# Longer rows for two streams of stores: the zero fill of a sum buffer, and the edge filters

## Chip, cores, metric
The kernel runs on one core of one Trainium2 chip. The metric is the device time of one execution in microseconds; the time given for a kernel is the median of its runs.

## What is computed
A graph of 10000 nodes with 512 features and 10000 edges goes through two layers, each with a residual and a normalisation over the features.

```python
def layer0(x):                      # graph convolution
    deg = segment_sum(w_all, dst_all);  norm = rsqrt(deg)[src] * w * rsqrt(deg)[dst]
    return relu(segment_sum((x @ W)[src_all] * norm, dst_all) + b)
x = layernorm(x + layer0(x))
def layer1(x):                      # message passing with edge filters
    h = softplus(edge_attr_20 @ Wf1 + bf1) - log 2
    filt = (h @ Wf2 + bf2) * edge_weight          # depends on the edges alone
    m = products of x[dst] @ W_in, edge directions and filt
    agg = segment_sum(m, src)                     # then small matrices per node
x = layernorm(x + layer1(x))
```

## The kernel before, in words
Edges and nodes are worked in tiles of 128 (79 live tiles; tensors are padded to 80). Five engines have an order of instructions each, written out by hand and tied by semaphores.

**Opening.** SP issues the small loads, then 33 fills of 512 KB (L421) and one of 256 KB (L422) that set `sum0` in HBM to zero; ScalarE's queue issues the first eight (`NZ`, L640). The source is `zeros`, 128 x 1024 fp32, so each fill writes 4 KB from each partition into two neighbouring rows of 2 KB. VectorE makes `zeros` by its first memset (L883). Meanwhile TensorE, VectorE and ScalarE compute the node degrees, and POOL gathers the first 12 tiles of x rows (L536).

**First edge stage** (some 84 to 340 us). A loop over groups `g` of four tiles: ScalarE and VectorE scale the gathered rows by the edge coefficient and split them into a high and a low part, TensorE sums rows with equal destination inside the group, ScalarE copies the sums to `R_mem` (L685), and POOL adds them to `sum0` by four indirect scatters (L552), then gathers four tiles for three groups later (L536). The scatters of a group wait until all of the group before have landed (`e_scat`), for the index columns that VectorE makes (`e_idx`, L991), and for the copy (`e_ev`). The first scatter also waits for the whole zero fill (`s_zero0`). In the same loop the filters of the second layer are made, since they depend on the edges alone: two tiles at a time, TensorE forms them (L1255), ScalarE writes them to `wst` (in `node_mem`, L679), and SP stores the pair to `filt_d` in HBM (L434), two stores of 512 KB per group. `wst[i % 4]` holds 128 partitions x 2 tiles x 512; the store puts tile v of the pair at rows 128 v + p, so that each row of 2 KB goes to a place of its own, 256 KB from the partition's other one.

**Node stage** (340 to 600 us), once all scatters have landed: x @ W0 and the first normalisation. **Second edge stage** (600 to 950 us): a loop over tiles with gathers, products, sums and scatters; SP loads the filter of tile t by `filt_in` (L456, 256 KB, four buffers), three tiles ahead. **Last stage**: the second normalisation and the output.

`keep` (128 x 6144) holds W0 in its first 2048 columns and, from the node stage on, part of x1.

Of the kernel before, what the change touches and what calls it, by code (L numbers as in the profile page):

```python
# [13 lines left out]
P = 128  # L14
# [3 lines left out]
D = 512  # L18
# [39 lines left out]
def place(t):  # L58

    g = (t + 2) // 3  # L60
    return g, t - first(g)
# [40 lines left out]

def rows(dram, t):
    return dram[bass.ds(t * P, P), :]


def pair_rows(dram, s, c0, c1):

    return dram[bass.ds(s * 2 * P, 2 * P), c0:c1].rearrange("(k p) d -> p k d", p=P)


def layer_pair(dram, j, c0, c1):
# [13 lines left out]
def build(nc, x, src_cols, dst_cols, src_row, weight, rbf, vec,  # L126
          W0, b0, Win_s, Win_v, Wf1, bf1, Wf2, bf2, W1_s, W1_v, W2_s, W2_v, out):
    sum0 = nc.dram_tensor("sum0", (NR + TRASH, D), F32, kind="Internal").ap()
    sum1 = nc.dram_tensor("sum1", (NR + TRASH, D), F32, kind="Internal").ap()
    x1_d = nc.dram_tensor("x1_d", (NR, D), F32, kind="Internal").ap()  # L130
    filt_d = nc.dram_tensor("filt_d", (NP, D), F32, kind="Internal").ap()

    with ExitStack() as ctx:
        def sb(name, shape, dt=F32):
            return ctx.enter_context(nc.sbuf_tensor(name, shape, dt))

        def sem(name):
            return ctx.enter_context(nc.semaphore(name))
# [7 lines left out]
        zeros = sb("zeros", [P, 1024])  # L146
# [33 lines left out]
        keep = sb("keep", [P, 24 * 2 * C])  # L180
# [26 lines left out]
        def views(start, n, width, mem=edge_mem):  # L207
            return [mem[:, start + i * width:start + (i + 1) * width] for i in range(n)]
# [24 lines left out]
        NG = 12  # L233
        G0 = G + [b[:, 2 * D:3 * D] for b in node_mem]
        junk1 = [b[:, 3 * D:3 * D + 3 * P] for b in node_mem]
        W0_s = [keep[:, c * D:(c + 1) * D] for c in range(4)]
        pick_even = views(0, 4, P)
        sl2 = [b[:, 0:2 * D] for b in node_mem]
# [7 lines left out]
        wst = [b[:, 0:1024].rearrange("p (v d) -> p v d", v=2) for b in node_mem]  # L246
        filt = [b[:, 0:512] for b in node_mem]
# [31 lines left out]
        s_zero = sem("s_zero")  # L279
        s_zero0 = sem("s_zero0")  # L280
# [63 lines left out]
        w_st = [sem(f"w_st{i}") for i in range(4)]  # L344
        w_dup = sem("w_dup")
        w_sidx = sem("w_sidx")
        f_filt = [sem(f"f_filt{i}") for i in range(4)]
# [32 lines left out]
        NZ = 8  # L380

        def zero_rows(j):
            return sum0[j * 256:(j + 1) * 256, :].rearrange("(p r) d -> p (r d)", r=2)
# [10 lines left out]

        minus = before[:, 0:P]

        block = ctx.enter_context(nc.Block())


        @block.sync  # L400
        def _(sp_):
# [14 lines left out]

            for s in range(2):
                sp_.dma_start(fT[s][:, :], rbf[:, s * Q:(s + 1) * Q]).then_inc(w_fT[s], 16)
            sp_.wait_ge(s_zero, 1)
            for j in range(NZ, 41):  # L420
                sp_.dma_start(zero_rows(j), zeros[:, :]).then_inc(s_zero0, 16)  # L421
            sp_.dma_start(sum0[41 * 256:, :], zeros[:, 0:D]).then_inc(s_zero0, 16)  # L422
            for c in range(4):
                sp_.dma_start(W0_s[c], W0[c * P:(c + 1) * P, :]).then_inc(s_wres, 16)
# [2 lines left out]
            for s in range(2, T4 + 3):  # L427
                if s < T4:
                    sp_.wait_ge(w_pre, s - 1)
                    sp_.dma_start(fT[s % 2][:, :], rbf[:, s * Q:(s + 1) * Q]).then_inc(w_fT[s % 2], 16)  # L430
                if s >= 3:
                    for i in (2 * (s - 3), 2 * (s - 3) + 1):
                        sp_.wait_ge(w_eva, 4 * (i + 1))
                        sp_.dma_start(pair_rows(filt_d, i, 0, D), wst[i % 4]).then_inc(w_st[i % 4], 16)  # L434


            sp_.wait_ge(e_lo, T)
# [15 lines left out]
                   .then_inc(f_trow[g % 4], 16)  # L453

            def filt_in(t):
                sp_.dma_start(filt[t % 4], rows(filt_d, t)).then_inc(f_filt[t % 4], 16)  # L456

            def nodes0(j):
                if j < T2:
                    if 1 <= j < 4:  # L460
                        x_in(j)
                    wait(sp_, n_tr, 2 * j - 6)
                    sp_.dma_start(in_pair(sl2[j % 4], j, 0, D), layer_pair(sum0, j, 0, D)).then_inc(n_sl[j % 4], 16)
                    if j == 4:
                        sp_.wait_ge(s_pairs, 1)
                    if j >= 8:
                        sp_.wait_ge(n_sum, 2 * j - 14)
                    if j >= 4:
                        x_in(j)
                if j >= 6:  # L470
                    i = j - 6
                    sp_.wait_ge(n_x1, min(2 * i + 2, TR - 2))
                    if i >= T2 - 2:
                        sp_.wait_ge(n_last, i - T2 + 3)
                    sp_.dma_start(layer_pair(x1_d, i, 0, D), in_pair(res2[i % 8], i, 0, D)).then_inc(n_st[i % 8], 16)
                    if i < T2 - 4:
                        sum1_out(i)
                    if i == T2 - 3:
                        sp_.wait_ge(n_tr, TR)
                        trow_in(0)  # L480
                        filt_in(0)
# [7 lines left out]
            for t in range(1, 4):  # L489
                filt_in(t)  # L490
                trow_in(t)
# [5 lines left out]
            for s in range(4, TR):  # L497
                g, j = place(s)
                if j == 0 and g >= 4:
                    sp_.wait_ge(f_M, first(g - 3))  # L500
                    trow_in(g)
                sp_.wait_ge(f_m, K_PROD * (s - 3))
                filt_in(s)
# [8 lines left out]
            for s in range(T2 + NA - 3):  # L512
# [4 lines left out]
                if s >= NA - 3:  # L517
                    t = s - NA + 3
# [8 lines left out]
        def _(pool):  # L527
# [6 lines left out]
            def gather0(t):  # L534
                k = t % NG
                pool.indirect_dma_start(G0[k], None, x, bass.IndirectOffsetOnAxis(ap=src_i[:, t:t + 1], axis=0)) \  # L536
                    .then_inc(e_gather[k // 4], 16)

            pool.wait_ge(s_load, 64)
            for t in range(NG):  # L540
                gather0(t)
            pool.wait_ge(s_zero0, 16 * 42)
            for g in range(T4):
                pool.wait_ge(e_idx, 2 * (g + 1))
                if g:
# [1 line left out]
                for n, j in enumerate((3, 2, 1, 0)):  # L547
                    t = 4 * g + j
# [44 lines left out]
            for g in range(G1 + 5):  # L593
# [7 lines left out]
                if g >= 5:  # L601
                    r = g - 5
# [272 lines left out]
        def _(dve):  # L875
# [5 lines left out]
                dve.wait_ge(s_const, count[0])  # L881

            dve.memset(zeros[:, :], 0.0).then_inc(s_zero, 1)  # L883
            dve.memset(eps_c[:, :], EPS)
            dve.memset(half_c[:, :], 0.5)
            dve.wait_ge(s_iota, 4)
# [48 lines left out]
            for s in range(T4 + 1):  # L935
# [18 lines left out]
                if s >= 1:  # L954
                    dve.wait_ge(s_look, g + 1)
                    for v in range(4):
                        t = 4 * g + v
# [16 lines left out]
                if s >= 1:  # L974
# [3 lines left out]
                    for q in (3, 2, 1, 0):  # L978
                        t, w = 4 * g + q, (q + 1) * P
                        dve.tensor_scalar(M[a][q], trow[a][:, 0:w], dst_f[:, t:t + 1], None, ALU.is_equal).then_inc(e_M, 1)  # L980
                    for n, q in enumerate((3, 2, 1, 0)):
                        t = 4 * g + q
# [26 lines left out]
            for q in range(2):  # L1009
                k = Y0 / (16.0 * C ** 0.5) if q == 0 else 1.0 / (16.0 * C ** 0.5 * 3.0 ** 0.5)  # L1010
# [7 lines left out]
            for k in range(2):  # L1018
                for half in range(2):
                    i = 2 * k + half  # L1020
# [65 lines left out]
            for t in (TR - 2, TR - 1):  # L1086
                g, k, r = t // 2, t % 2, res[t % 16]
# [378 lines left out]
```

## Time and profile before

| what | us |
|---|---|
| median of 3 runs (lowest, highest) | 1063.95 (1062.75, 1065.17) |
| the profiled execution | 1060.8 |
| its span from first to last instruction | 1058.7 |
| TensorE, VectorE, ScalarE, POOL busy | 943.4, 837.9, 703.7, 642.6 |
| SP's fills of `sum0`: first issue | 18.55 |
| shortest gather and shortest scatter on POOL | 0.95, 1.55 |

The span is what the views cover; the execution's own time holds some 2.1 us around it. A DMA share is the mean busy share of the core's 16 DMA engines in a stretch; overlapping packets can take it over 1. In a timeline the bracket gives how long the engine stood idle before the instruction, and what ended that by the semaphore events. A wait for several semaphores is put down to the last one that the profile saw.

### The profile page before, as it was taken

What the parts mean: (1) busy time and instruction counts of PE and PEld (TensorE: products, weight loads), DVE (VectorE), ACT (ScalarE), POOL (GpSimd) and SP (SyncE); (2) the same over time, 40 slices, a digit from 0 to 9 for tenths busy, and PEclk for the clock granted to TensorE, in tenths of its full rate; (3) what the DMA queues carried; (4) which work ended last, traced back from release to release, by engine and by line L of the source; (5) the groups of instructions that cost most, each with busy time, mean ns of one, the idle gap of its engine ahead of it and who ended that gap; (6) DMA issues with size and microseconds to landing.
All of it is one profiled execution on the core that took longest, in us unless ns stands there. A gap on an engine that the chain in (4) does not pass through costs nothing.

```text
span 1058.7 us, 17984 instructions
## 1 busy us (share of the span) xinstructions
PE 943.4 (89%) x5218; PEld 767.6 (73%) x5218; DVE 837.9 (79%) x2368; ACT 703.7 (66%) x1641; POOL 642.6 (61%) x931
## 2 busy tenths in 40 slices
PE   5979999898894999999999679999999999929885
PEld 4958777776673788888888457887888888818774
DVE  5778788887662789888888758888888888817998
ACT  2668877787682466666666645666666666618997
POOL 4017888888863356666666354676666766534664
PEclk9989999999896999999999889999999999969998
DMA  9989999999998599988999586999999999768999
GB/s 346 418 303 223 247 238 237 237 238 238 231 236 192 217 321 331 331 318 318 334 327 331 223 295 166 220 227 213 206 222 229 215 206 218 122 102 329 410 416 365
DMA packets 105703, 280.43 MB, mean 265 GB/s; under 512 B 13107, under 2 KB 17479, under 8 KB 105607
## 3 DMA queue, kind: packets, MB, share of 16 engines
q1 hardware_dynamic: 68598, 191.42, 49.3%
q0 software_dynamic: 35280, 82.63, 40.7%
q10 hardware_dynamic: 1728, 5.24, 1.3%
q8 instruction: 43, 0.70, 0.3%
q14 instruction: 54, 0.43, 0.1%
HBM read 132.38 MB, written 146.87 MB: 264 GB/s over the span
## 4 chain that ended last, share of the span: by engine, by line
PE 55%; DMA 6%; DVE 5%; issue 2%; ACT 1%; POOL 1%; SPq 0%; DVEq 0%; POOLq 0%; ACTq 0%
PE bank L1330 14%; PE bank L1334 7%; PE bank L1378 7%; PE bank L1361 7%; PE bank L1392 5%; PE bank L1390 3%; PE bank L1321 3%; PE bank L1355 3%; DVE stat L1168 2%; PE bank L1388 2%; PE bank L1367 2%; DMA out<-R_mem 1%; DMA sum<-R_mem,l_sidx 1%; PE bank L1365 1%; PE bank L1356 1%
## 5 line engine op out<-in xcount | busy, mean ns | idle before, releaser
L552 POOL DMA_INDIRECT sum<-R_mem,sidx_all x79 | 131.3, 1662 | 91.1 <-DMA sum<-zeros 49.3
L613 POOL DMA_INDIRECT sum<-R_mem,l_sidx x79 | 134.6, 1704 | 48.3 <-DMA sum<-R_mem,l_sidx 25.3
L1330 PE MATMUL bank<-G_hi 128*128 128x512 f32 x316 | 130.4, 413 | 0.0
L599 POOL DMA_INDIRECT G_mem<-x_d,dst_i x79 | 77.3, 979 | 87.3 <-PE bank L1365 61.5
L1330 PE MATMUL bank<-G_lo,G_hi 128*128 128x512 f32 x316 | 124.2, 393 | 0.0
L1244 PE MATMUL bank<-G_hi,M_mem 128*128 128x512 f32 x200 | 85.4, 427 | 9.4 <-ACT R_mem L685 9.4
L1334 PE MATMUL bank<-G_hi,G_lo 128*128 128x512 f32 x316 | 85.3, 392 | 0.0
L1119 DVE SCALAR_TENSOR_TENSOR edge_mem<-edge_mem,Y,bank 128x128 f32<-128x128 f32 x237 | 71.2, 385 | 15.1 <-ACT edge_mem L806 14.1
L1361 PE MATMUL bank<-edge_mem,Winv 128*128 128x512 f32 x158 | 81.8, 600 | 0.1
L1244 PE MATMUL bank<-G_lo,M_mem 128*128 128x512 f32 x200 | 79.6, 398 | 0.0
L1255 PE MATMUL bank<-edge_mem,Wf_s 128*128 128x256 f32 x320 | 78.6, 390 | 0.7 <-ACT node_mem L679 0.7
L754 ACT CAST G_hi<-bank 128x512 fp32r<-128x512 f32 x79 | 45.7, 579 | 40.5 <-PE bank L1321 40.2
L679 ACT ACTIVATE node_mem<-bank,bf_c 128x256 f32<-128x256 f32 x160 | 63.3, 490 | 13.5 <-issue 7.3
L1255 PEld LDWEIGHTS bank<-edge_mem,Wf_s 128*128 128x128 f32 x320 | 63.5, 201 | 11.6 <-issue 2.9
L584 POOL TENSOR_TENSOR node_mem<-node_mem,G_mem 128x512 f32<-128x512 f32 x40 | 53.6, 1339 | 28.9 <-ACT node_mem L768 28.9
L536 POOL DMA_INDIRECT G_mem<-x,src_i x55 | 58.2, 1059 | 20.7 <-issue 12.8
L1378 PE MATMUL bank<-G_hi,M_mem 128*128 128x512 f32 x157 | 68.4, 436 | 2.5 <-ACT R_mem L800 2.2
L1334 PEld LDWEIGHTS bank<-G_hi,G_lo 128*128 128x128 f32 x316 | 59.3, 188 | 13.1
L1330 PEld LDWEIGHTS bank<-G_lo,G_hi 128*128 128x128 f32 x316 | 59.6, 189 | 10.6
L1330 PEld LDWEIGHTS bank<-G_hi 128*128 128x128 f32 x316 | 59.5, 188 | 10.1
L1392 PE MATMUL bank<-MV,edge_mem 128*128 128x128 f32 x474 | 65.8, 275 | 0.0
L806 ACT COPY edge_mem<-bank 128x256 f32<-128x256 f32 x79 | 29.5, 373 | 53.9 <-issue 32.7
(263 smaller groups left out, 2921.2 us busy)
## 6 DMA issues: line engine op xcount, KB each, us to landing
node_mem<-sum SPq DMA_DIRECT2D x41, 512.0 KB, 5.9
filt_d<-node_mem SPq DMA_DIRECT2D x40, 512.0 KB
node_mem<-filt_d SPq DMA_DIRECT2D x79, 256.0 KB
sum<-zeros SPq DMA_DIRECT2D x33, 512.0 KB
G_mem<-x SPq DMA_DIRECT2D x20, 512.0 KB, 6.3
x_d<-node_mem SPq DMA_DIRECT2D x20, 512.0 KB, 2.9
sum<-node_mem SPq DMA_DIRECT2D x20, 512.0 KB, 4.5
edge_mem<-x SPq DMA_DIRECT2D x19, 512.0 KB, 6.3
```

The source lines that it names most:

```text
L552: pool.indirect_dma_start(sum0, bass.IndirectOffsetOnAxis(ap=sidx[:, t:t + 1], axis=0), R[t % 8][:, :], None, compute_op=ALU.add).then_inc ...
L599: pool.indirect_dma_start(G3[t % 8][:, :], None, x1_d, bass.IndirectOffsetOnAxis(ap=dst_i[:, t:t + 1], axis=0)) \
L613: pool.indirect_dma_start(sum1, bass.IndirectOffsetOnAxis(ap=l1_sidx[0:n, t:t + 1], axis=0), R3[t % 8][0:n, :], None, compute_op=ALU.add). ...
L679: act.activation(wst[i % 4][:, :, q * P:(q + 1) * P], bank[6 + q // 2][:, (q % 2) * 256:(q % 2 + 1) * 256].rearrange("p (v e) -> p v e", v=2),
L1119: st.mark(dve.scalar_tensor_tensor(mo[:, :, i], msg[c][:, 0:P], Y[:, bass.ds(t, 1), i], bank[6][:, i * P:(i + 1) * P], ALU.mult, ALU.add))
L1244: ins = pe.matmul(bank[b][:, :], M[c][q][:, j * P:(j + 1) * P], part_[(4 * g + q) % 8][:, :], start=(q == 3 and part_ is G_hi), stop=(q == ...
L1255: ins = pe.matmul(bank[6 + r][:, q * 256:(q + 1) * 256], Wf2_s[:, base:base + 255:2], h[c][:, v * 256:(v + 1) * 256], start=True, stop=True)
L1330: pe.matmul(bank[4 + a][:, :], zT_hi[a][:, c * P:(c + 1) * P], w[c][:, :], start=(c == 0 and w is W0h), stop=False)
L1334: ins = pe.matmul(bank[4 + a][:, :], zT_lo[a][:, c * P:(c + 1) * P], W0h[c][:, :], start=False, stop=(c == 3))
L1361: pe.matmul(bank[2][:, :], Winv[:, :], rawT[b][:, 0:512], start=True, stop=True)
L1378: ins = pe.matmul(bank[sum_bank[k]][:, :], M3[g % 3][j][:, k * P:(k + 1) * P], part_[t % 8][:, :], start=(k == j and part_ is msg_hi), sto ...
L1392: ins = pe.matmul(bank[6][:, i * P:(i + 1) * P], m[b][:, (3 + i) * P:(4 + i) * P], MV[:, 1, :], start=True, stop=True)
```

## The change
It has two parts. (1) A second memset makes `zeros_8k`, 2048 columns of zeros in columns 2048 to 4095 of `keep`. SP's 32 fills of 512 KB become 16 of 1 MB with 8 KB from each partition to four neighbouring rows; the 33rd, the 256 KB one and ScalarE's eight stay. SP waits for both memsets, and POOL for the new number of fills. (2) The two tiles of a filter pair are stored with their rows side by side: partition p's rows of tile 2i and 2i+1 are rows 256 i + 2p and 256 i + 2p + 1 of `filt_d`, so that a partition writes 4 KB in one piece. The load of a tile then reads every second row.

```diff
-def pair_rows(dram, s, c0, c1):
-    return dram[bass.ds(s * 2 * P, 2 * P), c0:c1].rearrange("(k p) d -> p k d", p=P)
...
+        zeros_8k = keep[:, 4 * D:8 * D]
...
+        def filt_pair(i):
+            return filt_d[i * 256:(i + 1) * 256, :].rearrange("(p v) d -> p v d", v=2)
...
-            sp_.wait_ge(s_zero, 1)
-            for j in range(NZ, 41):
-                sp_.dma_start(zero_rows(j), zeros[:, :]).then_inc(s_zero0, 16)
+            sp_.wait_ge(s_zero, 2)
+            for j in range(NZ // 2, 20):
+                sp_.dma_start(sum0[j * 512:(j + 1) * 512, :].rearrange("(p r) d -> p (r d)", r=4), zeros_8k).then_inc(s_zero0, 16)
+            sp_.dma_start(zero_rows(40), zeros[:, :]).then_inc(s_zero0, 16)
             sp_.dma_start(sum0[41 * 256:, :], zeros[:, 0:D]).then_inc(s_zero0, 16)
...
-                        sp_.dma_start(pair_rows(filt_d, i, 0, D), wst[i % 4]).then_inc(w_st[i % 4], 16)
+                        sp_.dma_start(filt_pair(i), wst[i % 4]).then_inc(w_st[i % 4], 16)
...
-                sp_.dma_start(filt[t % 4], rows(filt_d, t)).then_inc(f_filt[t % 4], 16)
+                sp_.dma_start(filt[t % 4], filt_pair(t // 2)[:, t % 2, :]).then_inc(f_filt[t % 4], 16)
...
-            pool.wait_ge(s_zero0, 16 * 42)
+            pool.wait_ge(s_zero0, 16 * (NZ + 18))
...
             dve.memset(zeros[:, :], 0.0).then_inc(s_zero, 1)
+            dve.memset(zeros_8k, 0.0).then_inc(s_zero, 1)
```

## Rows read from the trace of the kernel before

**Rows 1.** The page: busy time of each engine, and the count of DMA packets.
```profile
PE 943.4 (89%) x5218; PEld 767.6 (73%) x5218; DVE 837.9 (79%) x2368; ACT 703.7 (66%) x1641; POOL 642.6 (61%) x931
...
DMA packets 105703, 280.43 MB, mean 265 GB/s; under 512 B 13107, under 2 KB 17479, under 8 KB 105607
```

**Rows 2.** By stretch: length, engines' busy time, granted clock, DMA share, GB/s.
```profile
30.00:64.00 34.00, 29.85 (x128) 26.43 (x128) 22.91 (x92) 22.68 (x57) 0.00 (x0) 1.00 1.03 419
...
100.00:300.00 200.00, 182.22 (x889) 141.58 (x887) 158.13 (x578) 157.05 (x323) 163.23 (x120) 0.98 1.02 241
...
640.00:940.00 300.00, 293.02 (x1846) 235.50 (x1844) 254.34 (x735) 190.40 (x441) 193.11 (x140) 0.99 0.92 199
```

**Rows 3.** Timeline of POOL, first scatters: start, duration, instruction, idle before.
```profile
70.41 1.64 POOL L552 DMA_INDIRECT sum<-R_mem,sidx_all  x1 [49.30 <-DMA sum<-zeros]
...
79.03 1.55 POOL L552 DMA_INDIRECT sum<-R_mem,sidx_all  x1 [5.09 <-ACT R_mem L685]
```

**Rows 4.** Timeline of VectorE: memset, first work on loads, first index columns.
```profile
1.02 0.91 DVE L883 MEMSET zeros<- 128x1024 f32 x1 [1.02 <-PEq L1460]
...
5.67 0.20 DVE L891 CAST src_f<-src_i 128x80 f32<-128x80 int32 x1 [3.42 <-DMA rij<-vec]
...
69.44 0.16 DVE L991 TENSOR_TENSOR sidx_all<-off_all,dst_f 128x4 int32<-128x4 f32 x1
```

**Rows 5.** DMA view from 317.0 to 318.4 us.
```profile
DMA packets 259, 0.51 MB, mean 367 GB/s; under 512 B 8, under 2 KB 8, under 8 KB 259
...
q1 hardware_dynamic: 259, 0.51, 98.1%
```

**Rows 6.** DMA view from 30 to 64 us.
```profile
DMA packets 3904, 14.23 MB, mean 419 GB/s; under 512 B 434, under 2 KB 434, under 8 KB 3902
...
q1 hardware_dynamic: 3902, 14.21, 102.4%
```

**Rows 7.** Timeline of POOL in the first edge stage.
```profile
117.43 1.62 POOL L552 DMA_INDIRECT sum<-R_mem,sidx_all  x1 [0.30 <-issue]
...
123.10 1.99 POOL L552 DMA_INDIRECT sum<-R_mem,sidx_all  x1 [0.30 <-issue]
...
130.81 1.62 POOL L552 DMA_INDIRECT sum<-R_mem,sidx_all  x1 [0.30 <-issue]
...
297.26 1.55 POOL L552 DMA_INDIRECT sum<-R_mem,sidx_all  x1 [0.30 <-issue]
...
303.68 1.62 POOL L552 DMA_INDIRECT sum<-R_mem,sidx_all  x1 [0.71 <-issue]
```

**Rows 8.** By stretch, POOL with VectorE busy and with VectorE idle.
```profile
84.80:87.60 2.80, 2.80 (x14) 2.45 (x13) 2.61 (x9) 2.80 (x7) 2.39 (x2) 1.00 0.94 131
316.90:324.20 7.30, 6.28 (x29) 5.02 (x27) 0.00 (x0) 4.08 (x10) 6.23 (x4) 1.00 0.94 212
```

**Rows 9.** Timeline of POOL at the stage's end; last row: the chain of waits.
```profile
309.61 2.09 POOL L552 DMA_INDIRECT sum<-R_mem,sidx_all  x1 [0.30 <-issue]
316.99 1.56 POOL L552 DMA_INDIRECT sum<-R_mem,sidx_all  x1 [5.29 <-ACT R_mem L685]
...
322.58 1.56 POOL L552 DMA_INDIRECT sum<-R_mem,sidx_all  x1 [0.30 <-issue]
329.63 1.56 POOL L552 DMA_INDIRECT sum<-R_mem,sidx_all  x1 [5.50 <-issue]
...
333.36 5.75 DMA sum<-R_mem,sidx_all
```

**Rows 10.** The filter loads (L456): starts, and who waited for them.
```profile
L456 SPq DMA_DIRECT2D node_mem<-filt_d x79: 319/320/1595, 601.4 to 910.8; - x79
...
  DVE edge_mem L1128: 0.3, 1
```

**Rows 11.** Timeline of TensorE in the opening.
```profile
18.75 0.72 PE L1217 MATMUL bank<-hot_hi,hot_mem 128*128 128x80 f32 x2 [1.21 <-issue]
21.92 0.69 PE L1217 MATMUL bank<-hot_hi,hot_mem 128*128 128x80 f32 x2 [2.45 <-issue]
```

## The prediction
> **What bounds the kernel now.** I read the page first. TensorE is busy 943.4 of 1058.7 us, VectorE 79%, POOL 61% [rows 1]: near full on the whole, and an average says nothing of a single stage. The table by stretch does [rows 2]. From 345 us on, where the node and the second edge stage run, TensorE is the full one (293.02 of 300 us from 640 to 940) and the change touches only the reads of the filters there. The change works ahead of that: the zero fill (30 to 64 us: DMA share 1.03, 419 GB/s) and the first edge stage, where the filters are stored (100 to 300 us: share 1.02 at only 241 GB/s, TensorE 182 of 200). So the question is what sets the pace of these two.
>
> The timeline of POOL answers the first [rows 3]. Its first scatter starts at 70.41 after 49.30 us of idling that the profile puts down to the zeros. That looks like a 49 us prize, and is none: the index that the same scatter needs is written by VectorE at 69.44 for 0.16 us, to 69.60 [rows 4]. With the usual 0.30 us of dispatch the scatter could start at 69.90 at best. The third then waits 5.09 us for a sum that ScalarE copies, whose inputs come from TensorE and VectorE and not from the fill. From 84 us on POOL issues without a gap: in its timeline each instruction is preceded by 0.30 us of dispatch and hardly ever more, up to 310 us [rows 7], in groups of four scatters and four gathers, 13.38 us each (117.43 to 130.81). The stage then ends in three groups without gathers between them, where POOL waits for the scatters before to land, 5.29 and 5.50 us, and the last landing, 5.75 us, releases the node stage [rows 9]. That is what the end hangs on: POOL's issuing, then three landings.
>
> **The change, part by part.**
> *The wider memset.* VectorE's memset of 1024 columns takes 0.91 us, so one of 2048 takes about 1.82. It stands behind the first, in front of work that waits until 5.67 us for a load with 3.42 us of idling [rows 4]. Cost 0; without that cover it would be 1.82 us, and I see none of it left. SP's wait for it is free too: SP comes to it only after its weight loads, at 18.55 us (the table above).
>
> *What a packet costs.* From 317.0 to 318.4 us hardly anything but filter stores was under way: 98.1% of 16 engines for 1.40 us over 251 packets of 2 KB (259 less 8 small ones) are 87.5 ns each [rows 5]. From 30 to 64 us the queue carried 4 KB packets: 102.4% of 16 engines for 34 us over 3468 are 160.6 ns [rows 6]. Two of 2 KB cost 175.0, so a pair saves 14.4 ns, 8.2%. A store of 512 KB has 16 packets an engine now (1.40 us) and then 8 (1.285): 0.115 us less each, 0.23 us for the two of a group, 4.6 us for all 40. The other bound is 0, if what limits is bytes or if the long rows go out in pieces.
>
> *The zero fill.* 32 fills of 512 KB become 16 of 1 MB, 4 KB rows become 8 KB ones. The 32 take 32 x 1.285 = 41.1 us of full engines. No row shows an 8 KB data packet. The lower bound is 0. The upper takes the same 14.4 ns off each pair: 2 x 160.6 - 14.4 = 306.8 instead of 321.2 ns, 4.5%, 1.85 us. I take the nearer half of that, about 1 us, as true of the fill, and 0.0 on the path: only 0.51 us of it can reach the first scatter (70.41 to 69.90), and the third scatter's 5.09 us of idling take that up. ScalarE's eight fills keep their rows.
>
> *The filter stores in the stage.* They lie beside POOL's issuing. In steady groups the last scatter ends its issue at 123.10 + 1.99 = 125.09 and the next group's first starts at 130.81; less 0.30 of dispatch that is a cover of 5.42 us for the landing [rows 7]. At 303.68, with three gathers between, the landing shows through: 298.81 to 303.38, 4.57 us, with 0.71 us of idling instead of 0.30. So a faster store buys at most 0.41 there, and the like in the few other groups that show more than 0.30; I take 0.2 in all. Is POOL itself held up by the DMA? Its scatters take 1.55 us at least and up to 2.09 [rows 9]. While VectorE was idle and the DMA full of scatters and stores (316.9 to 324.2, share 0.94) four of them took 6.23 us, the minimum each; while VectorE was busy and the DMA moved 131 GB/s (84.8 to 87.6), two gathers took 2.39 us together where 0.95 is the least for one [rows 8]. The stretched ones go with the engines' work rather than with the DMA. So 0 from there.
>
> *The tail.* Two of the three landings, 311.70 to 316.69 (4.99 us) and 324.14 to 329.33 (5.19), have stores among them; the last has none [rows 9]. If two stores' packets stand ahead of each, they save 0.23 us each: 0.46.
>
> *The reads.* 79 loads of 256 KB keep their 2 KB rows, now 4 KB apart in memory. A row of 2 KB is its own packet either way. Only 0.3 us of waiting in the whole stage is put down to them [rows 10], and they are asked for three tiles ahead, some 11.9 us when 79 of them start from 601.4 to 910.8, 3.97 us apart. Cost 0; a cost would need loads that take several us more.
>
> **The sum.** 0 (memset) - 0 (fill) - 0.2 (loop) - 0.46 (tail) = about -0.7 us. In the profiled execution 1060.8 us (span 1058.7 and 2.1 around it) becomes 1060.1. The runs' median stands 3.15 us above it, at 1063.95, and becomes 1063.3.
>
> What the Trainium skill says of packets, in "DMA: Bandwidth & Descriptors" under "Why small descriptors are slow", is an overhead of about three cycles on a packet of one cycle per 32 bytes: 134 cycles for two of 2 KB against 131, 2.2% where the rows show 8.2%. By it a store would save an estimated 0.03 us and the sum would be about -0.2.
>
> **The rivals.**
> *The DMA sets the pace of the stage (faster).* For it: share 1.02 over 200 us, and a period of 13.38 us that is hardly more than the DMA could do. Against it: the two stretches of [rows 8] and a POOL that never idles. The 17 groups between 84 and 310 us would each give back 0.23, 3.9 us, the tail 0.46: 1063.95 - 4.4 = 1059.5.
>
> *Longer turns of the stores (slower).* A store's packets alternate with those of the scatters on each engine. Where a scatter's eight packets per engine take turns with a store's, each now waits behind 160.6 ns instead of 87.5: 8 x 0.073 = 0.58 us later landing. In steady groups the landing (5.19 in the tail) has 0.23 us to spare under the cover of 5.42, so 0.35 us show in each group in which the last scatter meets a store, and 0.58 in two landings of the tail. In all 17 groups that makes 6.0 + 1.2 = 7.2 us, in half of them 4.2: 1068.2. It decides once a landing takes over 5.42 us. Against it: the store's total work shrinks, and a store that meets the first three scatters delays the last one no more than now. The skill's rule for this is in the same page, "Queues, rings and completion order": an engine goes round its queues a packet at a time. The trace shows stores and scatters in the same stretches but not their turns.
>
> *Longer turns of the fill (slower).* TensorE stood 1.21 and 2.45 us at 18.75 and 21.92 us for nothing that the profile shows, with the DMA full [rows 11]. If code or some other small transfer is what it waits for, and packets of the fill are twice as long, these could double: +3.7, 1067.6. Against it: the same full DMA from 25 to 64 us shows no such gaps, and the fill only begins at 18.5.
>
> *The packets don't change.* If rows of 4 and 8 KB go out in the old pieces, nothing moves: 1063.95.
>
> **How the numbers follow.** Forecast 0.52; packets unchanged 0.10; DMA pace 0.20; turns of the stores 0.13; turns of the fill 0.05. Runs of this kernel lie within 1.2 us of their median, and 0.2% (2.1 us) is about what can be told from no change. Of the forecast's own spread (1061.5 to 1065.0) I put 0.03 beyond on the faster and 0.02 on the slower side. Faster by over 0.2%: 0.20 + 0.03 = 0.23. Slower: 0.13 + 0.05 + 0.02 = 0.20. Same: 0.57. The range reaches down to the DMA-bound case, 1059.5, and up to 1067.0, short of the two slower ones.
>
> **What the profile after would show.** Packets fewer by 40 x 128 = 5120 for the stores and 16 x 128 = 2048 for the fill (105703 to about 98,500) if the rows go out whole. The first scatter at 69.9 to 70.4, the third where it was. POOL's period still near 13.4 us with 0.30 ahead of each instruction; if it drops to 13.15, the DMA was the bound and I am wrong. Landings of 4.8 to 5.0 us in the tail; 5.5 and more with idling ahead of each group's first scatter would be the longer turns. The stages from 340 us on the same length: a longer one would speak against the reads.

## The result and the profile after

The changed kernel takes 1068.4 us (median of 6, 1066.67 to 1070.46) against 1063.14 us for the kernel before in the same series (6 runs): a ratio of 1.0049, 95% interval 1.0035 to 1.0063. It is about 5 us slower, outside the stated range (1059.5 to 1067.0) and on the side that was given 0.20. The rival "longer turns of the stores" had named 1068.2, from a start at 1063.95.

The page after, beside [rows 1]; lines behind L885 have moved by one, L552 has not:

```profile
span 1067.4 us, 17969 instructions
...
PE 949.4 (89%) x5218; PEld 773.7 (72%) x5218; DVE 839.2 (79%) x2369; ACT 703.4 (66%) x1641; POOL 643.6 (60%) x931
...
DMA packets 98279, 280.43 MB, mean 263 GB/s; under 512 B 12851, under 2 KB 17223, under 8 KB 96135
```

The engines' instruction counts are the same but for one memset. TensorE's busy time is 6 us longer, but it is 947.4 to 949.8 in runs below that lose nothing (fill alone, second store), so it does not mark the loss. The packets are fewer by 7424, the 7168 of the forecast and 256 small ones, so rows of 4 and 8 KB do go out whole. By stretch (beside [rows 2]) and in the DMA view from 30 to 64 us (beside [rows 6]):

```profile
30.00:64.00 34.00, 30.24 (x129) 26.83 (x128) 22.82 (x93) 22.52 (x58) 0.00 (x0) 1.00 1.01 426
100.00:300.00 200.00, 182.04 (x882) 142.37 (x881) 157.49 (x574) 154.60 (x316) 160.85 (x118) 0.97 1.01 238
```

```profile
DMA packets 1987, 14.48 MB, mean 426 GB/s; under 512 B 220, under 2 KB 220, under 8 KB 220
...
q1 hardware_dynamic: 1985, 14.46, 101.0%
```

The fill did get faster: 101.0% of 16 engines for 34 us over 1765 large packets are 311.3 ns for 8 KB, against 321.2 for two of 4 KB; 426 GB/s instead of 419. The first edge stage moved less in the same 200 us, 238 GB/s instead of 241. POOL's timeline tells where it stopped (beside [rows 3, 7, 9]):

```profile
70.99 1.64 POOL L552 DMA_INDIRECT sum<-R_mem,sidx_all  x1 [50.08 <-DVE sidx_all L992]
...
78.93 1.55 POOL L552 DMA_INDIRECT sum<-R_mem,sidx_all  x1 [4.42 <-ACT R_mem L685]
82.93 1.55 POOL L552 DMA_INDIRECT sum<-R_mem,sidx_all  x1 [2.46 <-ACT R_mem L685]
...
137.55 1.55 POOL L552 DMA_INDIRECT sum<-R_mem,sidx_all  x1 [0.30 <-DMA sum<-R_mem,sidx_all]
139.40 1.02 POOL L536 DMA_INDIRECT G_mem<-x,src_i  x1 [0.30 <-issue]
...
143.37 0.95 POOL L536 DMA_INDIRECT G_mem<-x,src_i  x1 [0.30 <-issue]
145.35 1.61 POOL L552 DMA_INDIRECT sum<-R_mem,sidx_all  x1 [1.04 <-issue]
...
246.27 1.56 POOL L552 DMA_INDIRECT sum<-R_mem,sidx_all  x1 [0.30 <-issue]
...
254.30 1.61 POOL L552 DMA_INDIRECT sum<-R_mem,sidx_all  x1 [0.75 <-issue]
...
308.61 1.61 POOL L552 DMA_INDIRECT sum<-R_mem,sidx_all  x1 [2.11 <-issue]
...
321.80 1.56 POOL L552 DMA_INDIRECT sum<-R_mem,sidx_all  x1 [5.54 <-issue]
...
334.87 1.56 POOL L552 DMA_INDIRECT sum<-R_mem,sidx_all  x1 [5.93 <-issue]
...
338.60 1.58 POOL L552 DMA_INDIRECT sum<-R_mem,sidx_all  x1 [0.30 <-issue]
```

The opening is as it was: the scatter now waits for VectorE's index and no longer for the zeros, and the first group's last scatter starts at 82.93. From there on a new idle stretch stands ahead of the first scatter of a group. The scatter that ended its issue at 137.55 + 1.55 = 139.10 has landed only at 145.05 (145.35 less 0.30), after 5.95 us; the one at 247.83 took until 254.00, 6.17 us. Here the four gathers cover 5.21 and 5.72 us, and the rest shows. Eight groups between 104 and 309 us show more than 0.30: 0.92, 0.65, 1.04, 1.01, 0.53, 0.71, 0.75 and 2.11, together 5.32 us over the dispatch. The kernel before shows 0.43, 0.64 and 0.71, or 0.88 us over; so its landings were not all below 5.42 either: these three took 5.89, 5.59 and 4.57 us. The difference of 4.4 and two waits longer by 0.25 and 0.43 us in the tail are 5.1; the stage's last scatter is issued at 338.60 instead of 333.36, 5.24 us later. (That this equals the difference of the medians is in part chance: these two executions differ by 8.7 us in their spans, see the end of the account below.) "issue" is what the bracket says, since the semaphore that POOL waits for is that of its own scatters; the place in the code (a group's first scatter, the one that waits for `e_scat`) tells that it is the landing.

The trace's semaphore events bear it out. Eight of the runs below have all 1264 increments of `e_scat`, 64 to a group. In them a first scatter with such an idle stretch starts 0.72 to 0.77 us after the group's 64th increment, whether the profile says "issue", VectorE or the DMA; only ahead of three second groups, where it names ScalarE's copy, is it longer.

### The profile page after: what moved, and what is told of

Read it like the earlier page. It is cut to its first block, busy times and chain, and to the rows that moved or that the text cites. A ratio compares the mean times of both kernels' runs of the same rounds, so it can differ in the third digit from the quotient of the medians.

```text
span 1067.4 us, 17969 instructions
## 1 busy us (share of the span) xinstructions
PE 949.4 (89%) x5218; PEld 773.7 (72%) x5218; DVE 839.2 (79%) x2369; ACT 703.4 (66%) x1641; POOL 643.6 (60%) x931
## 3 DMA queue, kind: packets, MB, share of 16 engines
q10 hardware_dynamic: 1728, 5.24, 1.3%
## 4 chain that ended last, share of the span: by engine, by line
PE 54%; DVE 6%; DMA 4%; issue 2%; ACT 1%; POOL 1%; SPq 0%; DVEq 0%; POOLq 0%; ACTq 0%
PE bank L1331 14%; PE bank L1335 7%; PE bank L1379 7%; PE bank L1362 6%; PE bank L1393 5%; PE bank L1391 3%; PE bank L1322 3%; DVE stat L1169 3%; PE bank L1356 3%; PE bank L1389 2%; PE bank L1368 2%; DVE node_mem L1160 1%; DMA sum<-R_mem,l_sidx 1%; PE bank L1366 1%; PE bank L1357 1%
## 5 line engine op out<-in xcount | busy, mean ns | idle before, releaser
L552 POOL DMA_INDIRECT sum<-R_mem,sidx_all x79 | 129.2, 1635 | 96.3 <-DVE sidx_all L992 50.1
L1245 PE MATMUL bank<-G_hi,M_mem 128*128 128x512 f32 x200 | 87.9, 439 | 12.3 <-ACT R_mem L685 12.3
L1245 PE MATMUL bank<-G_lo,M_mem 128*128 128x512 f32 x200 | 82.2, 411 | 0.0
L679 ACT ACTIVATE node_mem<-bank,bf_c 128x256 f32<-128x256 f32 x160 | 63.0, 486 | 13.9 <-PE bank L1256 10.3
L1256 PEld LDWEIGHTS bank<-edge_mem,Wf_s 128*128 128x128 f32 x320 | 64.1, 202 | 10.7 <-issue 2.1
L1379 PE MATMUL bank<-G_hi,M_mem 128*128 128x512 f32 x157 | 68.3, 435 | 2.5 <-issue 1.2
L1331 PEld LDWEIGHTS bank<-G_lo,G_hi 128*128 128x128 f32 x316 | 60.0, 190 | 10.7
L1331 PEld LDWEIGHTS bank<-G_hi 128*128 128x128 f32 x316 | 60.0, 190 | 10.3
```

The costliest lines, as they stand in the source:

```text
L552: pool.indirect_dma_start(sum0, bass.IndirectOffsetOnAxis(ap=sidx[:, t:t + 1], axis=0), R[t % 8][:, :], None, compute_op=ALU.add).then_inc ...
L679: act.activation(wst[i % 4][:, :, q * P:(q + 1) * P], bank[6 + q // 2][:, (q % 2) * 256:(q % 2 + 1) * 256].rearrange("p (v e) -> p v e", v=2),
L1245: ins = pe.matmul(bank[b][:, :], M[c][q][:, j * P:(j + 1) * P], part_[(4 * g + q) % 8][:, :], start=(q == 3 and part_ is G_hi), stop=(q == ...
L1256: ins = pe.matmul(bank[6 + r][:, q * 256:(q + 1) * 256], Wf2_s[:, base:base + 255:2], h[c][:, v * 256:(v + 1) * 256], start=True, stop=True)
L1331: pe.matmul(bank[4 + a][:, :], zT_hi[a][:, c * P:(c + 1) * P], w[c][:, :], start=(c == 0 and w is W0h), stop=False)
L1379: ins = pe.matmul(bank[sum_bank[k]][:, :], M3[g % 3][j][:, k * P:(k + 1) * P], part_[t % 8][:, :], start=(k == j and part_ is msg_hi), sto ...
```

## The experiments

Each ran beside the kernel before on the same chip, 5 rounds each, in four series; ratios may be compared between series, times may not (the kernel before stood at 1056.5 to 1062.0). "Idle over" is my sum from each POOL timeline as above: idle time over 0.30 us ahead of each group's first scatter, from the third group (at 99 to 105 us) to 312 us, leaving out waits that the profile gives to another engine (two of these, 1.45 us with the first store in 4 KB and 1.41 with stores of 1 KB, both at 101 us and given to VectorE, are landings too by the events). The two profiles above have 0.9 (before) and 5.3 (after). Between runs without a loss it goes from 0.5 to 2.8, so a difference of 2 us in it says nothing.

| run | fill | filter stores | hold | ratio (95% interval) | idle over, us |
|---|---|---|---|---|---|
| fill alone | 8 KB | 2 KB | no | 0.9992 (0.9972 to 1.0013) | 1.6 |
| filters alone | 4 KB | 4 KB | no | 1.0043 (1.0021 to 1.0066) | 6.6 |
| new places, 2 KB | 4 KB | 2 KB | no | 0.9992 (0.9973 to 1.0010) | 1.8 |
| 4 KB and hold | 4 KB | 4 KB | yes | 1.0004 (0.9984 to 1.0024) | 1.1 |
| first store 4 KB | 4 KB | 4 KB, 2 KB | no | 1.0045 (1.0021 to 1.0069) | 5.7 |
| second store 4 KB | 4 KB | 2 KB, 4 KB | no | 1.0005 (0.9986 to 1.0024) | 2.2 |
| before and hold | 4 KB | 2 KB | yes | 0.9995 (0.9979 to 1.0011) | 2.7 |
| whole change and hold | 8 KB | 4 KB | yes | 0.9983 (0.9963 to 1.0002) | 2.8 |
| the same again | 8 KB | 4 KB | yes | 0.9997 (0.9981 to 1.0014) | 0.8 |
| stores of 1 KB | 4 KB | 1 KB | no | 1.0002 (0.9987 to 1.0017) | 0.5 |
| new loads alone | 4 KB | 2 KB | no | 0.9990 (0.9967 to 1.0014) | 2.2 |
| new stores, old loads | 4 KB | 4 KB | no | 1.0030 (1.0010 to 1.0050) | 5.2 |

**Which half: the fill alone.** The kernel before with the first part of the diff.

> The fill alone: 8 KB rows for SP's fills, filter stores and loads as before. Turns of the stores: the stage keeps its landings, POOL starts its first scatter of a group after 0.30 us almost always, last scatter of the stage issued near 333.4 us, time 1063 us (within 2 us of before). Turns of the fill: gaps of TensorE in the opening grow and the time is 1067 to 1068.

0.9992: no loss, and no gain that can be measured. The turns of the fill are out as a cause.

**Which half: the filters alone.** The second part of the diff on the kernel before.

> The filters alone: stores in 4 KB rows and loads of every second row, fill as before. Turns of the stores: all of the loss is here, 1067 to 1069 us, with 0.5 to 1 us of idling ahead of the first scatter in several groups and two landings of 5.2 to 5.9 us at the end of the stage. Turns of the fill: 1063.

1.0043, the whole loss within the measurement. Its timeline of POOL, some of the first scatters of a group (L550 is the scatter's line here):

```profile
146.45 1.62 POOL L550 DMA_INDIRECT sum<-R_mem,sidx_all  x1 [0.69 <-issue]
...
213.94 1.62 POOL L550 DMA_INDIRECT sum<-R_mem,sidx_all  x1 [1.28 <-issue]
227.72 1.62 POOL L550 DMA_INDIRECT sum<-R_mem,sidx_all  x1 [0.89 <-issue]
...
308.21 1.62 POOL L550 DMA_INDIRECT sum<-R_mem,sidx_all  x1 [2.17 <-issue]
```

**Packet or place: neighbouring rows in packets of 2 KB.** Rows 2304 bytes apart are near each other as in the change, but not one run of memory.

```diff
-    filt_d = nc.dram_tensor("filt_d", (NP, D), F32, kind="Internal").ap()
+    filt_d = nc.dram_tensor("filt_d", (NP, D + 64), F32, kind="Internal").ap()
...
-            return filt_d[i * 256:(i + 1) * 256, :].rearrange("(p v) d -> p v d", v=2)
+            return filt_d[i * 256:(i + 1) * 256, 0:D].rearrange("(p v) d -> p v d", v=2)
```

> As the filters alone, but with rows of the filter buffer 2304 bytes apart, so that a pair's rows are neighbours yet leave in packets of 2 KB. Turns of the stores: packets are short again, so landings are as before and the time is 1063 to 1064. If it is where the rows lie in memory, or the loads of every second row, that costs: 1067 to 1069 as with the filters alone.

0.9992. With 2 KB packets the new places cost nothing that can be measured; in the whole loop only two groups show more than a few hundredths over the dispatch:

```profile
210.68 1.93 POOL L550 DMA_INDIRECT sum<-R_mem,sidx_all  x1 [0.93 <-issue]
...
304.58 1.61 POOL L550 DMA_INDIRECT sum<-R_mem,sidx_all  x1 [1.51 <-issue]
```

**Work or meeting: 4 KB packets, held until the scatters have landed.** The filters alone, with one wait more on SP.

```diff
                         sp_.wait_ge(w_eva, 4 * (i + 1))
+                        if s >= 4:
+                            sp_.wait_ge(e_scat, 64 * (s - 3))
                         sp_.dma_start(filt_pair(i), wst[i % 4]).then_inc(w_st[i % 4], 16)
```

> As the filters alone (4 KB packets), but SP holds a group's two stores until the scatters of the group before have landed, so that no store can stand among the last scatters before a landing that POOL waits for. Turns of the stores: idling ahead of a group's first scatter goes back to about 0.30 us, the two landings in the tail shrink towards the 4.2 us of one without stores, time 1061 to 1064. If the stores cost by their total work or by where they write, holding them changes nothing: 1067 to 1069.

1.0004: the loss is gone with the same packets, the same bytes and the same places. SP's timeline shows what moved. These are the two stores of a group (merged, from the first one's start to the second's end), in the kernel before, after and with the hold, in a group of the steady stretch; the last row is POOL's, the group's last scatter in the kernel before:

```profile
139.47 7.46 SPq L434 DMA_DIRECT2D filt_d<-node_mem  x2
```

```profile
139.37 7.43 SPq L434 DMA_DIRECT2D filt_d<-node_mem  x2
```

```profile
141.21 4.22 SPq L434 DMA_DIRECT2D filt_d<-node_mem  x2
```

```profile
136.49 1.97 POOL L552 DMA_INDIRECT sum<-R_mem,sidx_all  x1 [0.30 <-issue]
```

Before, the first store goes out 1.01 us behind the end of the last scatter's issue (138.46). After, it goes out at 139.37, 0.27 us behind (139.10), and in the group at 246.27 it is 1.1 us by the same timelines. So the store also came nearer to the scatter, and nearness is a rival of its own; the landings by size of packet, below, part the two. With the hold the last scatter's issue ends at 137.00 and the store goes out at 141.21, when those scatters are down: a landing of at most 4.21 us with no store of its own group beside it. POOL of that run in the same place, and its two tail landings:

```profile
135.03 1.97 POOL L552 DMA_INDIRECT sum<-R_mem,sidx_all  x1 [0.30 <-issue]
...
142.73 1.62 POOL L552 DMA_INDIRECT sum<-R_mem,sidx_all  x1 [0.30 <-issue]
...
315.36 1.56 POOL L552 DMA_INDIRECT sum<-R_mem,sidx_all  x1 [4.76 <-issue]
...
327.79 1.56 POOL L552 DMA_INDIRECT sum<-R_mem,sidx_all  x1 [5.29 <-issue]
```

142.73 follows 137.00 by 5.73 us with 0.30 of idling: the landing is again inside the cover. The waits in the tail are 4.76 and 5.29 us, against 5.12 and 5.55 with the filters alone, so they shrank by less than expected. The hold has a price, too: the stage's last landing, from the start of its scatter, takes 6.62 us here and 6.68 to 6.92 in the three other runs with it, against 5.20 to 5.85 in all runs without.

**Which store: only the first of a group's two in 4 KB packets, then only the second.**

```diff
-            return filt_d[i * 256:(i + 1) * 256, :].rearrange("(p v) d -> p v d", v=2)
+            rows_ = "(p v) d -> p v d" if i % 2 == 0 else "(v p) d -> p v d"
+            return filt_d[i * 256:(i + 1) * 256, :].rearrange(rows_, v=2)
```

> Fill as before; only the first of a group's two filter stores leaves in 4 KB packets, the second in 2 KB packets at the old places. By the timelines the first store is issued within 1.5 us of the end of the group's last scatter's issue, so its packets meet that scatter's. Turns of the stores: most of the loss stays, 1065 to 1068, with 0.5 to 1 us of idling ahead of the first scatter of several groups. If 4 KB packets cost by their number alone: half the loss, about 1064.5, the same as its sister run.

> Only the second store of a group leaves in 4 KB packets; it is issued some 6 us later, while the next group's first scatters are still to be issued or just issued, with three more behind them. Turns of the stores: little or no loss, 1061 to 1063.5, idling ahead of a group's first scatter about 0.30 us as before. By number alone: about 1064.5.

1.0045 and 1.0005. The two have the same number of packets (103142 by their pages) and the same bytes, and differ in the moment at which the large ones are under way. (1.0045 is 1063.73 us, under the 1065 expected, because the kernel before took 1059.68 in this series.) Four rows of each, first scatters of a group (L551 here):

```profile
129.96 1.62 POOL L551 DMA_INDIRECT sum<-R_mem,sidx_all  x1 [0.61 <-issue]
143.66 1.62 POOL L551 DMA_INDIRECT sum<-R_mem,sidx_all  x1 [0.99 <-issue]
157.66 1.62 POOL L551 DMA_INDIRECT sum<-R_mem,sidx_all  x1 [1.25 <-issue]
171.32 1.62 POOL L551 DMA_INDIRECT sum<-R_mem,sidx_all  x1 [0.64 <-issue]
```

```profile
210.27 1.61 POOL L551 DMA_INDIRECT sum<-R_mem,sidx_all  x1 [0.34 <-issue]
223.61 1.84 POOL L551 DMA_INDIRECT sum<-R_mem,sidx_all  x1 [0.57 <-issue]
237.08 1.62 POOL L551 DMA_INDIRECT sum<-R_mem,sidx_all  x1 [0.37 <-issue]
290.96 1.62 POOL L551 DMA_INDIRECT sum<-R_mem,sidx_all  x1 [0.46 <-issue]
```

The semaphore events give every group's landing, also where the gathers hide it: from the end of the last scatter's issue to the group's 64th increment. (Counted so it is 0.46 us shorter than from the idle stretches above, so the cover of 5.42 is one of 4.96 here.) These are my means over the groups, third to seventeenth, in which the first store was issued between 0.2 us before and 0.9 us behind that end, in runs with all increments and without the hold:

| first store | run | groups | landing (lowest, highest), us |
|---|---|---|---|
| 1 KB | stores of 1 KB | 8 | 4.50 (4.00, 5.08) |
| 2 KB | new loads alone | 8 | 4.84 (4.64, 5.06) |
| 2 KB | second store 4 KB | 9 | 4.96 (4.49, 5.23) |
| 4 KB | first store 4 KB | 6 | 5.46 (4.92, 5.84) |
| 4 KB | new stores, old loads | 11 | 5.19 (3.80, 5.77) |

At like distance from the scatter the landing grows with the store's packets, by 0.50 us from 2 to 4 KB in the one pair of the same series and by 0.35 in the other. Nearness alone does not make the loss.

**The hold by itself.** The same wait on the kernel before.

> The kernel before, with the hold of SP alone (2 KB packets). Turns of the stores: the landings of before mostly hide already, only the tail and two or three groups can gain, 0 to 2 us: 1060 to 1062. If the hold by itself is what made the 4 KB run as fast as before (by 5 us or so), it shows here as 1057.

0.9995: the hold gains nothing that can be measured where packets are of 2 KB, so in the 4 KB run it did not win 5 us of its own; it took away the loss.

**The whole change with the hold, twice.**

> The whole change (8 KB fill, 4 KB stores) with the hold. Turns of the stores: the loss is gone, 1060 to 1063, level with the kernel before or up to 2 us under it. If the fill and the stores together cost something that neither does alone: above 1064.

> The whole change with the hold once more, since its first interval ended just at no change. A real gain of 1 to 2 us shows again as 0.998 to 0.999; a ratio of 1.000 or more would say that there is none.

0.9983 and 0.9997. The loss is gone here too. A gain over the kernel before isn't shown: both intervals take in 1.

**Shorter turns: stores of 1 KB.** The filter buffer is laid out in half rows with 256 bytes between them; stores and loads move 1 KB pieces.

```diff
+    filt_d = nc.dram_tensor("filt_d", (2 * NP, D // 2 + 64), F32, kind="Internal").ap()
...
+            return filt_d[i * 512:(i + 1) * 512, 0:D // 2].rearrange("(p v) d -> p v d", v=4)
```

> Fill as before; the filter stores, and the filter loads with them, in packets of 1 KB. Turns of the stores: turns are shorter still, the idling ahead of first scatters is as before or less, and the stage ends no later; only the packets' fixed cost grows (some 0.12 us a store, hidden under POOL): time within 2 us of before. If what hurts is any change of the packet size or the stores' total work on the DMA engines: slower, by 2 us or more.

1.0002, with little idling (one group at 0.76, and the first wait of 1.41 named above). Four times as many store packets as with 4 KB cost nothing that can be measured, and the landings of the table are the shortest. That what counts is how long each packet holds an engine fits this; it is not shown.

**The loads.** Two runs part the loads from the stores. In both, stores and loads no longer agree on the rows, so a filter falls to another edge; the work is the same.

```diff
-                sp_.dma_start(filt[t % 4], rows(filt_d, t)).then_inc(f_filt[t % 4], 16)
+                sp_.dma_start(filt[t % 4], filt_d[(t // 2) * 256:(t // 2) * 256 + 256, :].rearrange("(p v) d -> p v d", v=2)[:, t % 2, :]).then_inc(f_filt[t % 4], 16)
```

> The stores and the fill as before, only the filter loads take every second row (the rows then belong to other edges, so this leaves the filters mixed up; the work is the same). If the loads are free, as forecast: within 2 us of before, and from the last scatter of the first edge stage to the end 725 to 728 us. If rows 4 KB apart cost in the second edge stage: 1 to 3 us slower, with that stretch longer.

> The stores in 4 KB packets, the loads as before (again with the filters mixed up). If the loads are free: the whole loss stays, ratio near 1.0045. If they carry part of it: 1.002 to 1.004.

0.9990 for the new loads alone, 1.0030 for the new stores with the old loads. By its expectation 1.0030 lies where the loads would carry part of the loss. But its interval, 1.0010 to 1.0050, takes in the 1.0043 of both together, and the new loads alone cost nothing that can be measured. So the stores carry the loss, whole or most of it.

## Why the prediction was wrong, by its steps

*The bound of the stage* was read rightly: POOL's issuing, then three landings. So was the price of packets: 311.3 ns for 8 KB where the upper bound said 306.8, and 3.1% of the fill saved, 1.3 us of 41.1. By the cycles of the Trainium skill ("DMA: Bandwidth & Descriptors", "Why small descriptors are slow") that pair would save an estimated 1.1%; the measured 3.1% lies between this and the forecast's upper bound of 4.5%.

*The wider memset, the fill on the path, the reads*: 0 each, as found within the measurement. The fill alone is at 0.9992, the loads alone at 0.9990, and the first scatter's wait passed to VectorE's index as the sum had it.

*The step that failed* is the pair of terms "0.2 (loop) and 0.46 (tail)" saved. They took a store that meets a scatter for a matter of total work: less work, earlier landing. The forecast then set its own rival aside with "the store's total work shrinks, and a store that meets the first three scatters delays the last one no more than now". In place of that the runs show that the store which counts is the one issued just behind the last scatter, and that 4 KB packets in it delay the landing more than 2 KB packets do, though by the price of a packet the store has less work in all. In the loop, what shows of a landing went from three groups to eight, at 5.81 to 6.38 us, where 5.19 + 0.58 had given 5.77, and the idling grew by 4.4 us instead of shrinking by 0.2; the rival had about 3.0 for half the groups. The size of the effect was 0.35 to 0.50 us a landing by the table, for the rival's 0.58. The slack was smaller than its 0.23: landings with 2 KB stores close behind took 4.84 and 4.96 us under a cover of 4.96 by the same count. In the tail the forecast's 0.46 saved is not seen, and the rival's 1.2 lost is not either. The two waits there add up to 10.8 us before and 11.5 after, but to 10.7, 10.6 and 10.3 in the three other runs with an unheld first store of 4 KB, and to 10.2 to 10.9 in four of the five others without the hold (13.3 in the fifth, the loads alone). That 1068.2 stands so near the measured 1068.4 is in part luck: the rival's sum was 4.2 us over 1063.95, the measured difference 5.3 over 1063.14.

*The weight was wrong more than the arithmetic.* The terms in the forecast's favour came to 0.7 us, bounded in the loop by what was exposed (0.41 us in the group it read). Against them stood 0.23 us of slack, under 17 groups. With so little to win and every group able to lose, the slower side deserved more than 0.20.

*The DMA-bound rival*, at 0.20, is out: a stage whose pace the DMA sets would have gained from cheaper packets, and in most groups POOL stood idle before for no more than the 0.30 us of dispatch.

What stays open: the turns themselves. No view shows the order of packets on an engine; what is shown is that the loss needs 4 KB packets and needs the first store to be among the last scatter's packets. The Trainium skill ("DMA: Bandwidth & Descriptors", "Queues, rings and completion order") says that an engine goes round its queues a packet at a time; this fits all twelve runs and is not proved by them. The packet of that page typically holds some 9 to 17 descriptors, and no run here shows that it is the packet which the profile counts, as the prediction took it to be. Another reason for a longer hold of the engine by the larger packet would look the same.

Open, too, is where the rest of the loss arises. The profiled execution also stands 3.5 us longer behind the last scatter (338.60 to 1067.4 against 333.36 to 1058.7). This stretch is 727.5 to 728.8 us in the four runs that lose, 726.7 with the second store in 4 KB, and 725.2 to 726.1 in the five others without the hold; with the hold it is 726.9 to 728.4, some 1 us of it the longer last landing. So of the losing runs' time some 2 us lies behind the stage, behind all filter stores. From the second group's first scatter (at 85 to 91 us) to the last scatter the losing profiles take 245.3 to 248.3 us, those of the five others 241.7 to 245.3. The mean granted clock over a run was 0.960, 0.958 and 0.957 in three of the kernels that lose (filters alone, first store in 4 KB, new stores with old loads) against 0.962, 0.962 and 0.960 of the kernel before beside them. Whether that is the cause of the 2 us or a sign of it no run tells.

## What to carry to other kernels

Before making a transfer's packets longer, look for what shares the DMA engines with it and for whose landing somebody waits. Here the price was 0.35 to 0.50 us on such a landing, and it was paid because the landing had less slack than that. A background transfer that got cheaper gained nothing here, since it was hidden, and still lost. If the long packets are wanted, issue them after the landing that matters; one wait on the queue that issues them was enough here, and as it made another landing some 1 us longer, it won nothing beyond the loss.

## What the runs showed of the hardware

An 8 KB row leaves as one packet: 1765 large packets in 34 us for 14.46 MB, 426 GB/s on one queue of stores from SBUF to HBM. And the size of a plain store's packets, at the same bytes and within the same 1.1 us of issue, moved the mean landing of an indirect scatter beside it from 4.84 and 4.96 us (2 KB) to 5.19 and 5.46 (4 KB), counted from the end of the issue to the semaphore's last increment.
